# Graph layer kernel: 13 dense blocks and 25 gathered groups in place of 11 and 29

## What is computed

```
norm_out, norm_in = clip(out_degree, 1)**-0.5, clip(in_degree, 1)**-0.5
h = x
for _ in range(3):                                   # three hops
    agg = segment_sum((h * norm_out[:, None])[src], dst)
    h = 0.5 * (agg * norm_in[:, None]) + 0.5 * x
y = layernorm(x + h @ W.T)
e = relu(concat(y[src], y[dst]) @ W1 + b1)           # one row for each edge
w = sigmoid(e @ W2 + b2)
att = y + segment_sum(w * y[src], dst)
out = layernorm(y + layernorm(att) * gamma + beta)
```

## Time and profile before

| | |
|---|---|
| median of 3 runs | 1218.95 us (1218.7 to 1220.7) |
| profiled execution | 1217.36 us |
| its span, first to last instruction | 1215.6 us |
| mean granted TensorE clock | 0.917 |
| PE busy | 957.0 us (79%) |
| PEld busy | 779.0 us (64%) |
| DVE busy | 943.2 us (78%) |
| ACT busy | 567.3 us (47%) |
| POOL busy | 658.3 us (54%) |

### The profile page before, as it was taken

The page is one execution under the profiler, slowest core; times in us unless marked ns, Lnnn a source line. Parts: engine busy times, 40 slices in busy tenths (PEclk is TensorE's granted clock), DMA queues, the critical chain, the costliest instruction groups (busy, mean ns, idle before and its releaser), DMA issues.

```text
span 1215.6 us, 33073 instructions
## 1 busy us (share of the span) xinstructions
PE 957.0 (79%) x11099; PEld 779.0 (64%) x11100; DVE 943.2 (78%) x2559; ACT 567.3 (47%) x1391; POOL 658.3 (54%) x789
## 2 busy tenths in 40 slices
PE   3766666688889989995699888888888887888860
PEld 2666566567777877784487666666666666666650
DVE  7988888799999988884699777676666767666766
ACT  6555555631100002222577555555555555555556
POOL 2000000036766435766777777777777777777721
PEclk9999999989999999998699889788788979888885
DMA  3000000000000001112776666666665666665511
GB/s 95 1 0 0 0 0 0 1 2 2 2 3 2 3 2 33 41 49 65 227 210 202 193 184 185 182 181 181 177 188 177 187 181 191 179 187 176 176 33 54
DMA packets 77399, 120.08 MB, mean 99 GB/s; under 512 B 20632, under 2 KB 39628, under 8 KB 77260
## 3 DMA queue, kind: packets, MB, share of 16 engines
q0 software_dynamic: 22272, 60.85, 17.9%
q1 hardware_dynamic: 54988, 57.44, 15.7%
HBM read 111.41 MB, written 6.81 MB: 97 GB/s over the span
## 4 chain that ended last, share of the span: by engine, by line
POOL 37%; DVE 24%; PE 18%; issue 16%; ACT 3%; DMA 1%; DVEq 1%; POOLq 0%; SPq 0%; ACTq 0%
POOL region L928 25%; POOL U L928 8%; PE bank L1785 7%; DVE stage L1034 5%; PE bank L1670 4%; POOL stage L928 3%; PE bank L1672 2%; PE bank L1746 2%; DVE stage L1197 2%; DVE aggT L1034 2%; DVE aggT L1217 1%; DVE t L1285 1%; ACT region L2013 1%; DVE stage L1210 1%; DVE U L1294 1%
## 5 line engine op out<-in xcount | busy, mean ns | idle before, releaser
L928 POOL DMA_INDIRECT region<-src_split,region x320 | 309.0, 966 | 97.4 <-issue 96.8
L1785 PE MATMUL bank<-U,region 128*128 128x256 f16 (+1 forms) x1875 | 235.3, 276 | 3.8 <-DVE U L1174 2.1
L1785 PEld LDWEIGHTS bank<-U,region 128*128 128x128 fp8e4 x1875 | 178.9, 98 | 35.8 <-DVE U L1174 2.8
L1391 DVE SCALAR_TENSOR_TENSOR region<-bank,PQ 128x512 f16<-128x512 f32 x116 | 80.0, 690 | 129.3 <-ACT PQ L2142 129.0
L2049 ACT CAST region<-bank 128x500 f32 x202 | 119.9, 593 | 92.2 <-PE bank L1672 68.2
L2142 ACT ACTIVATE PQ<-bank 128x512 f16<-128x512 f32 x116 | 69.3, 597 | 197.7 <-PE bank L1823 196.5
L2171 ACT CAST region<-bank 128x512 f16<-128x512 f32 x286 | 152.9, 591 | 0.0
L1670 PE MATMUL bank<-stage 128*128 128x175 f16 x544 | 92.9, 256 | 48.6 <-DVE aggT L1034 25.3
L928 POOL DMA_INDIRECT U<-src_split,region x108 | 104.4, 966 | 32.9 <-issue 32.6
L1457 DVE SCALAR_TENSOR_TENSOR region<-bank,region 128x512 f16<-128x512 f32 x143 | 98.5, 689 | 25.2 <-ACT region L2151 24.3
L781 POOL MEMSET region<- 128x1875 uint8 x1 | 1.7, 1662 | 212.8 <-ACT region L2049 212.8
(11 more groups left out here) (292 smaller groups left out, 2372.3 us busy)
## 6 DMA issues: line engine op xcount, KB each, us to landing
region<-slot_rows SPq DMA_DIRECT2D x143, 256.0 KB
region<-in_dst_dram SPq DMA_DIRECT2D x116, 64.0 KB
region<-src_split,region POOLq DMA_INDIRECT x320
region<-tgt_split SPq DMA_DIRECT2D x116, 16.0 KB
U<-src_split,region POOLq DMA_INDIRECT x108
src_split<-U SPq DMA_DIRECT2D x25, 64.0 KB, 1.5
src_split<-xs SPq DMA_DIRECT2D x25, 64.0 KB, 1.5
tgt_split<-q SPq DMA_DIRECT2D x25, 64.0 KB, 1.6
```

The costliest lines, as they stand in the source:

```text
L928: nc.gpsimd.indirect_dma_start(out=rows_of(n, i), out_offset=None, in_=src_split, in_offset=bass.IndirectOffsetOnAxis(ap=listed[n % LISTS] ...
L1785: z = nc.tensor.matmul(bank[2 * (k % 2) + p][:, 0:width], count[:, h, b * P:(b + 1) * P], U[k % 2][:, h, 0:width], start=h == 0, stop=h == ...
```

## The change

Two more target blocks go from gathered to dense: FIRST_BLOCK 14 becomes 12, so DENSE is 13, HALF_BLOCKS 26, TOTAL (units) 169 and STEPS 175; POOLED 29 becomes 25, so 100 batches. LAST_GROUPS is again seven groups, now of 4, 4, 4, 1, 4, 4, 4 blocks (before 4, 4, 3, 4, 4, 4, 2).

The sort's half block hs has its scan in hop block `sorted_at(hs)` = 3 + 63 hs // 25 (3, 5, 8, 10, 13, ... 63, 66) instead of every third block; the later parts keep their distances of 2, 4, 6 and 7 blocks. Since parts of several half blocks can now fall in one hop block, `sort_vector` takes the places first, then the numbers, then the scan. GpSimd's and SP's calls follow the same list.

ohJ and ohW are laid out with the two tiles of a pair innermost, so that L1430 and L1407 have steps of one element in all their 16-bit operands but the target column, and `sums` reads every second element of ohW.

```diff
--- before.py
+++ after.py
@@ -49,9 +49,9 @@
     DEEP = 3
 
 
-    POOLED = 29
+    POOLED = 25
     BATCHES_POOLED = POOLED * BPS
-    FIRST_BLOCK = 14
+    FIRST_BLOCK = 12
     DENSE = NB - FIRST_BLOCK
     LISTS = 4
     RING = 3
@@ -103,6 +103,15 @@
         n, left = divmod(at - first, every)
         return n if left == 0 and 0 <= n < end else None
 
+    def sorted_at(hs):
+
+        return 3 + hs * (2 * NB + 13) // (HALF_BLOCKS - 1)
+
+    def sort_of(s, lag):
+        return next((hs for hs in range(HALF_BLOCKS) if sorted_at(hs) + lag == s), None)
+
+    assert all(sorted_at(hs + 1) - sorted_at(hs) >= 2 for hs in range(HALF_BLOCKS))
+
     def tiles_in(n):
         return min(TPS, TILES - n * TPS) if isinstance(n, int) else TPS
 
@@ -171,7 +180,7 @@
-        ohJ = [carve(region, taken, [TPS, JW], f16) for _ in range(2)]
+        ohJ = [carve(region, taken, [TPS // 2, JW, 2], f16) for _ in range(2)]
@@ -339,7 +348,7 @@
-        ohW = [sb(f"ohW{i}", [P, TPB // 2, 2, 2, JW], f16) for i in range(3)]
+        ohW = [sb(f"ohW{i}", [P, TPB // 2, 2, JW, 2], f16) for i in range(3)]
...
@@ -907,9 +916,9 @@
                   .then_inc(pq_split, 1)
             for c in range(NB + 2):
                 split(c, c % 2)
-                n = due(c, 2, 3, HALF_BLOCKS - ahead + 2)
-                if n is not None:
-                    sort_ahead(ahead + n, ahead + n + 1)
+                for hs in range(ahead, HALF_BLOCKS + 2):
+                    if sorted_at(hs) == 2 * NB + 7 + c - 2:
+                        sort_ahead(hs, hs + 1)
 
             g.wait_ge(slots_psum, HALF_BLOCKS)
             g.wait_ge(slots_stored, 64 * HALF_BLOCKS)
@@ -1242,15 +1251,15 @@
 
             def sort_vector(s):
                 judge_input(s)
-                hs = due(s, 3, 3, HALF_BLOCKS)
+                hs = sort_of(s, 4)
+                if hs is not None:
+                    sort_places(hs)
+                hs = sort_of(s, 2)
+                if hs is not None:
+                    sort_numbers(hs, s)
+                hs = sort_of(s, 0)
                 if hs is not None:
                     sort_scan(hs)
-                hs = due(s, 5, 3, HALF_BLOCKS)
-                if hs is not None:
-                    sort_numbers(hs, s)
-                hs = due(s, 7, 3, HALF_BLOCKS)
-                if hs is not None:
-                    sort_places(hs)
 
             def scaled_sums(k, b, p, factor, plus, link):
 
@@ -1406,9 +1415,9 @@
-                    ohJ[n % 2][:, q * TPB:(q + 1) * TPB, :].rearrange("p (a t) j -> p a t j", t=2).unsqueeze(2)
-                    .broadcast_to([P, TPB // 2, 2, 2, JW]),
-                    weight_parts[s % 2][:, 0:TPB // 2, :, :].unsqueeze(4).broadcast_to([P, TPB // 2, 2, 2, JW]), ALU.mult).then_inc(ohw_ready, 1)
+                    ohJ[n % 2][:, q * TPB // 2:(q + 1) * TPB // 2, :, :].unsqueeze(2)
+                    .broadcast_to([P, TPB // 2, 2, JW, 2]),
+                    weight_parts[s % 2][:, 0:TPB // 2, :, :].unsqueeze(3).broadcast_to([P, TPB // 2, 2, JW, 2]), ALU.mult).then_inc(ohw_ready, 1)
@@ -1428,8 +1437,9 @@
-                    ohJ[p][:, :, :], iota[:, 0:JW].unsqueeze(1).broadcast_to([P, TPS, JW]),
-                    jT[:, n * TPS:(n + 1) * TPS].unsqueeze(2).broadcast_to([P, TPS, JW]),
+                    ohJ[p][:, :, :, :], twice[:, 0:JW, :].unsqueeze(1).broadcast_to([P, TPS // 2, JW, 2]),
+                    jT[:, n * TPS:(n + 1) * TPS].rearrange("p (a t) -> p a t", t=2).unsqueeze(2)
+                    .broadcast_to([P, TPS // 2, JW, 2]),
@@ -1758,19 +1768,19 @@
-                hs = due(s, 5, 3, HALF_BLOCKS)
+                hs = sort_of(s, 2)
-                hs = due(s, 9, 3, HALF_BLOCKS)
+                hs = sort_of(s, 6)
-                hs = due(s, 10, 3, HALF_BLOCKS)
+                hs = sort_of(s, 7)
-            offs_before = sum(due(s, 5, 3, HALF_BLOCKS) is not None for s in range(2 * NB))
-            fills_before = sum(due(s, 9, 3, HALF_BLOCKS) is not None for s in range(2 * NB))
-            turns_before = sum(due(s, 10, 3, HALF_BLOCKS) is not None for s in range(2 * NB))
+            offs_before = sum(sort_of(s, 2) is not None for s in range(2 * NB))
+            fills_before = sum(sort_of(s, 6) is not None for s in range(2 * NB))
+            turns_before = sum(sort_of(s, 7) is not None for s in range(2 * NB))
@@ -1858,7 +1868,7 @@
-                                             ohW[b % 3][:, i // 2, w_half, i % 2, :], start=i == 0 and y_half + w_half == 0,
+                                             ohW[b % 3][:, i // 2, w_half, :, i % 2], start=i == 0 and y_half + w_half == 0,
...
```

More of the change, by code:

```diff
@@ L656, in _ @@
                 tables(c, c % 2)
-                hs = due(2 * NB + c, 9, 3, HALF_BLOCKS)
+                hs = sort_of(2 * NB + c, 6)
                 if hs is not None:
@@ L866, in sort_ahead @@
                         judge(hs - 3)
-            ahead = (2 * NB - 1) // 3 + 2
+            ahead = next(hs for hs in range(HALF_BLOCKS) if sorted_at(hs) >= 2 * NB + 7)
             sort_ahead(0, 1)
```

## The result

| | before | after |
|---|---|---|
| median of 4 runs | 1219.13 us | 1171.66 us (1170.99 to 1174.88) |
| ratio after / before | | 0.961, 95% interval 0.960 to 0.963 |
| profiled execution (span) | 1217.36 (1215.6) | 1174.88 (1173.1) |
| mean granted TensorE clock | 0.917 | 0.939 |

Faster by 47 us in the medians; forecast was 1168. The profiled execution after is the slowest of its four, 3.2 us over their median, so the spans differ by 42.5 us only.

What follows compares the result with a forecast made beforehand. GpSimd's gathers were taken to bound the attention stage; gathers -81.2, ring start +6, other load +3, sort +20 and tail +1 gave -51 from 1217.36 us, hence 1166, and 1.6 more for the median: 1168 us, range 1149 to 1192.

Steps and rivals of the forecast that it cites:

- The gathers set the pace: Attention stage: GpSimd's gathers stay the bound; 400 instead of 464 at 1.269 us each take 81.2 us off the chain.
- Start of the ring: Attention stage's start: GpSimd stalls for TensorE's sums, 4 us at gather group 3 and 2 at group 4; bounds 0 and 12.
- "No other line between first and last gather in the chain": Sign expected in the attention stage: the chain of waits holds only L928's gathers, x400 at 1.27 us.
- Sort: Three hops: 26 half blocks instead of 22 add 7, 6.5 and 9 us, 22 in all, taken as 20; bounds 9 and 32.
- "VectorE is full, so its work counts whole": Hop 0: one scan step, one number step and two place steps more on VectorE add 7 us.
- The judge: GpSimd's nine-part check of the input's limits, in the hops; 4 us counted for its operations still falling in hop 1.
- Tail: After the last gather: one group less to add, but four blocks in the last group; +1 us, bounds -2 and +4.
- 1 (steps bind): Attention stage: the steps, not the gathers, set the pace in part; 21 us more, 1189; chance 0.16.
- 2 (cheap sort): Hops and ring start: the sort costs only 9 us and the start's stall is nil; 1151 us; chance 0.10.
- 3 (lock on gathers): Attention stage: every added L1441 stops a gather for its whole 0.366 us; 33 us instead of 3, 1198; chance 0.06.
- 4 (low clock): Attention stage: TensorE's lower clock becomes steady; 1204 us at 0.83, about 1228 at 0.78; chance 0.06.
- 5: One-hot weights: the new layout of ohW and ohJ is no faster; same time, counted within the forecast's 0.62.

Runs made afterwards that it cites:

- Size 11: The changed kernel with FIRST_BLOCK 11 and POOLED 23 instead of 12 and 25, two buffers some words longer; 1201.26 us, ratio 0.984.
- RAMP 8: The changed kernel with RAMP, the unit steps before a batch may join every step, 8 instead of 12; 1169.79 us, ratio 0.959.
- experiments 1 and 6: The changed kernel with ohJ and ohW in their old layout, 1171.31 us, and the changed kernel with RAMP 8, 1169.79 us.
- experiment 1: The changed kernel with ohJ and ohW in their old layout, all else of the change kept; 1171.31 us, ratio 0.961.

## Why the prediction was right, and where not

**The gathers set the pace: right.** 1.277 us each instead of 1.269 over 400: 3.3 us more, forecast 3. The mean is 974 ns (966 before). The size is right, its source only in part: the forecast put all of it down to L1441. In the trace after, the 70 gathers that had L1451 (that line) running beside them 0.1 us after their start took 1008 ns in the mean, but the 25 that had L1475, a tensor_tensor, took 1069 ns, and the 85 that had L1467, which reads PSUM, 945 ns. Size 11 shows how near the steps are: one more block, and GpSimd waits 15.6 us for slots.

**Start of the ring: right in kind and place, nearly in size.** One stall of 3.9 us at 666.3 us, before gather group 3, where 4 had been forecast; the 2 us for group 4 did not come. RAMP 8 removes it and gets 2.4 us of stage for it.

**"No other line between first and last gather in the chain": wrong.** The chain goes through TensorE's steps until about 790 us and along the gathers from 820. This is not for want of the 10% to spare: TensorE made a batch in 4.60 us up to batch 36, where the forecast had 4.58, and GpSimd gathered one in 5.2. But it started 29.9 us behind, and at some 0.6 us gained with each batch that takes about 200 us to work off. The forecast had both numbers and did not put them together. It cost nothing, since apart from the one stall GpSimd found its slots free.

**Sort: right in hops 1 and 2, 6 us short in hop 0.** The step that failed is "VectorE is full, so its work counts whole", with the four sort steps' own durations as the only addition. The judge was priced once, in hop 1, at its cost of before. Leaving it out shows 4.3 us of cost in hop 0 before and 10.8 after. Its number of operations there hardly rose: 14 of its 20 before, 16 after, GpSimd busy with them 28.7 and 29.2 us. VectorE's busy time is stretched by 6.6 us before and 9.3 after. The rest shows on TensorE: before, the judge adds 0.8 us to its busy time and 1.5 to its waits for scans; after, 5.4 (the clock is 0.92 with it and 0.97 without) and 5.5. So the same operations of GpSimd cost more where the sort leaves less slack; which of the two, stretch or clock, comes first is not shown. Over the three hops the judge's growth is 13.5 - 8.2 = 5.3 us, and the rest is 22.5 us, where the working gave 22 and was cut to 20. Executions with the same hops differ by 2 us (339.3 here, 337.2 in experiments 1 and 6), so the runs do not tell 22 from 20. Two slips in the working changed no result: hop 1 counts 5.4 us of VectorE for a half block whose operations add up to 5.64, which still fits under the 19.3 us taken for five blocks, and L1407 stands at 243 ns in the working and at 237 among the signs.

**Tail: 2.6 us short.** The last unit's L1467 starts 7.6 instead of 6.1 us after the last gather's end, the norms and stores of the last group of four blocks take 40.5 instead of 39.3, and between them the products that add the last sums (fp32, x8) take 2.09 instead of 1.17. The two chains:
```profile
1130.28 2.09 PE bank L1928 x8
```
```profile
1174.92 1.17 PE bank L1918 x8
```
The clock had fallen to 0.5 at 1130.14, just before them.

**Layout: nothing, as forecast, for one operation of two.** L1416 is at 242 ns (243 forecast). L1439 is at 482, not 317, as it is with the old layout (481 in experiment 1): its operand jT is f32, and the forecast looked at the steps alone. The Trainium skill (VectorE: DVE Perf Modes, "What auto-detection actually checks") asks, for the faster mode that two inputs can have, for 16-bit data and steps of one in every tensor of the operation. Both rows agree with it; that the f32 operand alone is the cause is argued, no run changed it.

**Rivals.** 1 (steps bind): not at 12, but at 11. 2 (cheap sort): no, hops +27.7. 3 (lock on gathers): no, the median stayed at 946 ns and the mean rose by 8. 4 (low clock): no, 0.94 to 1.00 in the middle of the stage. 5: half of it happened (L1439), unnoticed.

Sum of the misses: hops 7.7, tail 2.6, gathers with the ring's start -1.9, the rest 0.1: 8.5 us against a profiled execution that is itself 3.2 over its median. The profiled execution before was 1.6 under its median, which the forecast took for the difference again; these 4.8 us of scatter are why 1168 stands only 3.7 from 1171.66. That the number came so near is thus in part luck: the 6 us missed in hop 0 are a missed term, and the scatter between executions is nearly as large.

What stays open: why the casts waited out GpSimd's operation and L1310 only in part; and why the judge costs TensorE so much more after than before.

## What to carry to other kernels

When work moves from a stage bound by one engine to others, price the new load per pipeline block, not per stage: where three sort steps met, a block took 8 to 13 us, where most others took 3 to 7. A spread by integer division should be looked at for its shortest runs of gaps against the distances between dependent parts. And before a size is changed, try one step to either side: here 13, 12 and 11 give 1190, 1172 and 1201 us, with a different limit at each end.

## What the runs showed of the hardware

- GpSimd's elementwise work on 816 columns stretched VectorE's operations beside it: a cast from 0.21 to 1.63 us, 265 operations in hop 0 from 92.7 to 102.1 us. Eight casts that began during such a tensor_tensor of GpSimd all ended 0.08 or 0.09 us after it. Nine such parts cost 8 to 16 us wherever they were put, also in a stage where GpSimd was idle.
- The gathers' descriptor making hardly noticed VectorE: median 946 or 947 ns in every kernel, mean 974 beside 338 operations of 128x512. It depends on what VectorE runs as a gather starts: 1069 ns in the mean beside L1475, 1008 beside L1451, 945 beside L1467 and L1460.
- In the hops TensorE's granted clock fell with the bursts: 0.97 with the judge moved out of hop 0, 0.92 with it, 0.87 where three sort steps met. For nearly the same products TensorE was busy 91.3, 97.1 and 98.7 us.
